# List of slots in two halves, the first gathers issued beside the later searches, TensorE given work ahead of their end, the last expert's rows signalled by halves

## The reference, cut to what matters

```python
cap = int(CAP_FACTOR * T / E)                          # 140
topp, topi = jax.lax.top_k(probs, TOPK)
score = jnp.where(routed, probs, -jnp.inf)
idx = jnp.argsort(-score, axis=0)[:cap].T              # 32 lists of 140 token numbers
xe = xf[idx]                                           # gather
up = jnp.einsum('eci,eji->ecj', xe, w_up)
gate, upv = jnp.split(up, 2, axis=-1)
ye = jnp.einsum('ecj,eoj->eco', silu(gate) * upv, w_down)
out = jnp.zeros((T, C)).at[idx.reshape(-1)].add((w[..., None] * ye).reshape(-1, C))
```

## Time and profile before

| what | us |
|---|---|
| median of three timed runs | 810.26 |
| profiled execution, its time | 806.49 |
| its span | 804.7 |
| the searches (L669) | 21.9 |
| last search to the turn of expert 0's rows | 7.35 |
| turn of expert 0's rows to turn of expert 1's | 8.87 |
| turn of expert 1's rows to that of expert 2's | 7.95 |
| end of the last matmul of the last expert to the last add issued | about 5 |

### The profile page before, as it was taken

How to read it: one execution, slowest core, us unless ns; L and a number is a source line. 1 busy time by engine, 2 the same in 40 slices (tenths; PEclk the granted TensorE clock), 3 DMA queues, 4 the chain that set the end, 5 groups by cost and what they waited for, 6 DMA issues and landing times.

```text
span 804.7 us, 17481 instructions
## 1 busy us (share of the span) xinstructions
PE 675.4 (84%) x5198; PEld 532.4 (66%) x5198; DVE 507.6 (63%) x1371; ACT 393.2 (49%) x1590; POOL 322.9 (40%) x339
## 2 busy tenths in 40 slices
PE   7899999999999999998866111079999999999993
PEld 4456666666666666665643100069999999999992
DVE  5665777867777786766578888925454545454541
ACT  1467686867768686777732563012222222222220
POOL 3343453534445353441101000035656565656542
PEclk8999999999999999999976555579999999999997
DMA  5600020202002020101014200018898988898931
GB/s 163 238 1 24 25 70 2 70 26 69 24 23 70 2 69 24 46 1 46 2 41 133 74 1 0 0 33 258 245 274 253 266 243 272 251 274 234 278 60 14
DMA packets 57422, 84.44 MB, mean 105 GB/s; under 512 B 11282, under 2 KB 28304, under 8 KB 57360
## 3 DMA queue, kind: packets, MB, share of 16 engines
q1 hardware_dynamic: 47168, 73.04, 27.7%
q0 software_dynamic: 9216, 9.76, 7.4%
q10 hardware_dynamic: 976, 0.96, 0.4%
HBM read 71.04 MB, written 12.69 MB: 104 GB/s over the span
## 4 chain that ended last, share of the span: by engine, by line
PE 60%; DVE 17%; ACT 14%; issue 4%; DMA 2%; SPq 1%; POOL 1%; ACTq 0%; DVEq 0%; POOLq 0%
PE pair L808 19%; PE bank L818 10%; ACT arena L1083 7%; PE pair L1385 6%; DVE arena L1254 5%; PE pair L1394 3%; PE bank L1413 3%; PE bank L1352 3%; PE pair L1380 3%; DVE arena L669 3%; PE bank L1340 2%; PE bank L1345 2%; PE bank L828 2%; ACT arena L489 2%; PE bank L1364 1%
## 5 line engine op out<-in xcount | busy, mean ns | idle before, releaser
L1083 ACT ACTIVATE arena<-pair,arena 112x112 f32<-112x112 f32 x512 | 175.5, 365 | 72.3 <-DVE arena L1254 68.5
L808 PE MATMUL pair<-arena,we 128*128 128x140 f32 x1024 | 139.9, 285 | 0.7 <-ACT arena L729 0.6
L772 DVE SCALAR_TENSOR_TENSOR arena<-arena,pair 128x140 f32<-128x140 f32 x160 | 47.7, 298 | 133.8 <-issue 73.6
L714 POOL DMA_INDIRECT rows_out<-arena,slot_row x64 | 94.4, 1475 | 92.7 <-DVE arena L761 75.0
L808 PEld LDWEIGHTS pair<-arena,we 128*128 128x128 f32 x1024 | 130.1, 192 | 1.8 <-issue 1.8
L737 ACT ACTIVATE arena<-pair 128x140 f32<-128x140 f32 x160 | 45.9, 287 | 149.0 <-PE pair L808 99.0
L705 POOL DMA_INDIRECT arena<-rows,slot_row x64 | 62.5, 977 | 120.8 <-issue 120.8
L1083 ACT ACTIVATION_READ_ACCUMULATOR arena<-pair,arena 112x1 f32 x512 | 110.0, 215 | 0.0
L818 PE MATMUL bank<-arena,we 128*128 128x140 f32 x512 | 83.3, 286 | 0.0
L1254 DVE TENSOR_REDUCE arena<-pair 112x8 f32<-112x896 f32 x64 | 69.4, 1085 | 19.8 <-PE pair L1385 19.0
L1394 PEld LDWEIGHTS pair<-tab,arena 112*112 112x112 f32 x512 | 52.0, 134 | 30.6 <-issue 28.7
(11 more groups left out here) (188 smaller groups left out, 1178.5 us busy)
## 6 DMA issues: line engine op xcount, KB each, us to landing
we<-w_experts_in SPq DMA_DIRECT2D x192, 256.0 KB
wa<-w_adapters_in SPq DMA_DIRECT2D x16, 384.0 KB
arena<-ctx_in SPq DMA_DIRECT2D x8, 448.0 KB, 4.4
arena<-x_in SPq DMA_DIRECT2D x8, 448.0 KB, 3.8
rows_out<-arena SPq DMA_DIRECT2D x8, 448.0 KB, 3.3
rows<-arena SPq DMA_DIRECT2D x8, 448.0 KB, 3.4
arena<-rows,slot_row POOLq DMA_INDIRECT x64
rows_out<-arena,slot_row POOLq DMA_INDIRECT x64
```

Source lines behind the costliest of these rows:

```text
L714: nc.gpsimd.indirect_dma_start(d["out"], bass.IndirectOffsetOnAxis(ap=slot_row[:, h, e:e + 1], axis=0), yr[e % 2][:, h, :], None, compute_ ...
L772: signal(dve, nc.vector.scalar_tensor_tensor(gs[m % 2], th[m % 2], 1.0, banks[m % 4][:, 0:CAP], ALU.add, ALU.mult), s_gs, n + 1)
L808: last = nc.tensor.matmul(banks[m % 4][:, part * CAP:(part + 1) * CAP], w[:, col0:col0 + 128], xet[j % 2][:, c, :], start=(c == 0), stop=( ...
L1083: last = nc.scalar.activation(pr[s % 2][:, j, :], banks[BS[s % 4]][0:T, j * T:(j + 1) * T], ACT.Exp, bias=nmx[s // 2 % 2][:, s % 2, j:j + ...
```

## The change

`HALF` is 72, nine of the 18 searches. After the ninth, VectorE turns the first 72 columns into token numbers and signals `s_found`; TensorE adds them up into bank 5; two searches later VectorE writes the first half of `slot_row` and signals `s_slot`. GpSimd then issues the gathers of the first halves of experts 0 to 3, and after the second signal the second halves of the same four. The second half of the list goes into bank 6 and takes the same steps after the last search. Each search now scans only up to its own numbers (`place[:, 0:end]`, 904 to 1040 columns). Three searches (`WAKE`) before the end VectorE signals `s_wake`, on which TensorE runs two of the large matmuls; behind the second half of the list it runs five (`WARM // 2 - 1`) where it ran three. In `add` the two waits change places, and for the last expert each half of the rows is signalled on its own.

```diff
-        pe.wait_ge(s_found, 1)
         for h in range(2):
-            last = nc.tensor.matmul(banks[5][0:HC, h * NE:(h + 1) * NE], row_id[:, h * HC:(h + 1) * HC],
-                                    tab[:, TAB["chunk"]][:, 0:NE], start=True, stop=True)
-        last.then_inc(s_placed, 1)
+            if h == 1:
+                pe.wait_ge(s_wake, 1)
+                keep_warm(2, ident[0:T, 0:T], tab[0:T, 0:NT])
+            pe.wait_ge(s_found, h + 1)
+            nc.tensor.matmul(banks[5 + h][0:HC, 0:NE], row_id[:, h * HC:(h + 1) * HC],
+                             tab[:, TAB["chunk"]][:, 0:NE], start=True, stop=True).then_inc(s_placed, 1)
...
+        def rows_at(h):
+
+            some = slice(h * HALF, (h + 1) * HALF)
+            link(nc.vector.scalar_tensor_tensor(row_id[:, some], at[:, some], tab[:, TAB["first"]], shift[:, some], ALU.add,
+                                                ALU.subtract))
+            link(nc.vector.scalar_tensor_tensor(row_id[:, some], at[:, some], float(CHB * T), row_id[:, some], ALU.is_lt,
+                                                ALU.mult))
+            dve.sem_inc(s_found, 1)
+
+        def slots(h):
+            dve.wait_ge(s_placed, h + 1)
+            nc.vector.tensor_scalar(slot_row[:, h, :], banks[5 + h][0:HC, 0:NE], tab[0:HC, TAB["spare"]][:, h:h + 1], None,
+                                    ALU.add).then_inc(s_slot, 1)
+
         for i in range(FINDS):
             some = slice(i * FIND, (i + 1) * FIND)
-            last = nc.vector.max_index(at[:, some], place[:, CHB * T + i * FIND:CHB * T + (i + 1) * FIND], place)
+            end = CHB * T + (i + 1) * FIND
+            last = nc.vector.max_index(at[:, some], place[:, end - FIND:end], place[:, 0:end])
+            if (i + 1) * FIND == HALF:
+                link(last)
+                rows_at(0)
+            elif (i + 1) * FIND == HALF + 2 * FIND:
+                slots(0)
+            elif i == FINDS - 1 - WAKE:
+                link(last)
+                dve.sem_inc(s_wake, 1)
         link(last)
...
+        rows_at(1)
+        slots(1)
...
-            pool.wait_ge(s_yr, e + 1)
-            plain(pool)
             wait(pool, s_added, 32 * e)
             plain(pool)
+            pool.wait_ge(s_yr, e + 1)
+            plain(pool)
             for h in range(2):
+                if e == NE - 1 and h == 1:
+                    pool.wait_ge(s_yr, NE + 1)
                 nc.gpsimd.indirect_dma_start(d["out"], bass.IndirectOffsetOnAxis(
...
-        for e in range(4):
-            fetch(e)
+        for h in range(2):
+            pool.wait_ge(s_slot, h + 1)
+            for e in range(4):
+                fetch(e, h)
...
-            last.then_inc(s_yr, 1)
+                if halves or h == 1:
+                    last.then_inc(s_yr, 1)
...
-        pe.wait_ge(s_slot, 1)
-        keep_warm(WARM // 4, ident[0:T, 0:T], tab[0:T, 0:NT])
+        pe.wait_ge(s_slot, 2)
+        keep_warm(WARM // 2 - 1, ident[0:T, 0:T], tab[0:T, 0:NT])
```

More of the change, by code:

```diff
@@ L33 @@
 PAD = FIND * FINDS
+HALF = PAD // 2
+WAKE = 3
+assert HALF % FIND == 0 and HC <= HALF
 NCH, CHB = 4, NB // 4
@@ L448, in program @@
     s_counted, s_base, s_placed, s_found = sem("chosen_counted"), sem("bases"), sem("row_ids"), sem("rows_found")
-    s_slot = sem("slot_rows")
+    s_slot, s_wake = sem("slot_rows"), sem("search_nearly_done")
     s_cand, s_sc = sem("bounds"), sem("scalar_candidates")
@@ L665, in routing_vector @@
         link(nc.vector.tensor_tensor(place[:, 0:CHB * T], pg, pe_, ALU.add))
+        def rows_at(h):
[9 more added lines that the diff above has]
+                                    ALU.add).then_inc(s_slot, 1)
         for i in range(FINDS):
             some = slice(i * FIND, (i + 1) * FIND)
-            last = nc.vector.max_index(at[:, some], place[:, CHB * T + i * FIND:CHB * T + (i + 1) * FIND], place)
-        link(last)
[L671 to L679, removed]
+            end = CHB * T + (i + 1) * FIND
[8 more added lines that the diff above has]
+                dve.sem_inc(s_wake, 1)
+        link(last)
+        rows_at(1)
+        slots(1)
     s_xet, s_xrt, s_up, s_th, s_hh, s_yt, s_yts, s_yw, s_yr = (sem(n) for n in (
@@ L700, in experts_pool, with fetch @@
         pool.wait_ge(s_fo, 16 * 2)
[L701 to L706, removed]
+        def fetch(e, h):
+            nc.gpsimd.indirect_dma_start(xr[e % 4][:, h, :], None, d["rows"], bass.IndirectOffsetOnAxis(
+                ap=slot_row[:, h, e:e + 1], axis=0)).then_inc(s_xr[e % 4], 16)
         def add(e):
+            wait(pool, s_added, 32 * e)
+            plain(pool)
             pool.wait_ge(s_yr, e + 1)
             plain(pool)
-            wait(pool, s_added, 32 * e)
-            plain(pool)
             for h in range(2):
+                if e == NE - 1 and h == 1:
+                    pool.wait_ge(s_yr, NE + 1)
                 nc.gpsimd.indirect_dma_start(d["out"], bass.IndirectOffsetOnAxis(
@@ L722, in experts_pool @@
             if e + 4 < NE:
-                fetch(e + 4)
+                fetch(e + 4, 0)
+                fetch(e + 4, 1)
         pool.wait_ge(s_added, 32 * NE)
@@ L755, in experts_vector, with turned @@
     def experts_vector(dve, link):
-        def turned(e, j):
+        def turned(e, j, halves=False):
             dve.wait_ge(s_yw, e + 1)
@@ L788, in experts_vector @@
                 expert(4 * i + j, j, False)
-        turned(NE - 1, 3)
+        turned(NE - 1, 3, True)
     def experts_tensor(pe):
```

## The result

The changed kernel took 807.31 us in the median of 8 runs (804.70 to 810.42), the kernel before 810.41 in the median of its own 8. The ratio is 0.9962 with a 95% interval from 0.9945 to 0.9978: 3.1 us less, between 1.8 and 4.5. 808.4 had been forecast.

The account below looks back on a forecast made before the run. Experts bound by TensorE, searches by VectorE; gains lie in searches, the way to first rows, the clock's second fall and tail. Against the median 810.26: 0.45 + 1.0 + 0.45 = 1.9, so 808.4 us; range 805.9 to 810.6.

Parts of the forecast that it names:

- The searches and the list: Shorter scans save 1.28 us, work between searches adds 1.1, the end saves 0.6: slots complete 0.75 us earlier.
- The gathers: Early gathers leave one behind the last signal: expert 0's rows land 2.2 us earlier, most of it hidden behind five matmuls.
- rival 3: Searches and gathers disturb each other: slots 3.8 us later, time about 811.9; chance 0.04.
- Rival 4: First half not early because of another GpSimd wait; expert 0's second gather comes fifth, about 811.5; chance 0.03.
- The turn of expert 0's rows: Before the first expert, TensorE's five large matmuls delay the turn: 531.3, 0.45 us earlier than before.
- u: Time from the start of the five large matmuls to the clock's rise: 3.35 to 3.9 us, allowed 2.5 to 6.
- The formula: End of the five large matmuls behind the list: 525.75 + 3.73 + u/2.
- rival 2: Five matmuls outlast the rows; with first up blocks still at half clock, +1.0 us, 811.2; chance 0.10.
- The fall of the clock: Between the large matmuls and the second expert the clock no longer falls: 1.6 us gained against the profiled execution.
- The discount to 1.0: The clock-fall gain counted as 1.0 us against the median, since not each run of before need have the fall.
- The tail: Behind the last expert, the first add waits only for the first half of rows: 0.45 us saved, bounds 0 and 0.5.
- Rival 1: Early matmuls raise the clock before the five run: 3.7 to 4.3 us less, time 806.2; chance 0.27.

Follow-up runs that it names:

- before_tail: The kernel before with only the edit of the last expert's rows and the swapped waits; single run, last-step-to-first-add 1.33 us instead of 1.82, no timed ratio.
- the paced matmuls: Changed kernel with one large matmul signalled by each of the 12th to 17th searches instead of two at once; 804.90 and 806.10 us, ratios 0.9937 and 0.9946 to before.

## Why the prediction was right, point by point

**The searches and the list.** 0.75 us had been worked out to the start of the large matmuls; it was 0.64 (24.00 -> 23.36 us after the first search). The scan's 1.28 came as 1.27, and what is added less what is saved as 0.63 instead of 0.5.

**The gathers.** They ran beside the searches, ended before the second half, and disturbed nothing: seven searches took 8.32 us with them and 8.32 without. So rival 3, a port conflict, falls (its price, 3.8 us on top of the forecast, would have been 812.2 and not 811.9); this agrees with the Trainium skill's exemption for VectorE instructions with one SBUF input ("SBUF — State Buffer", Who interferes with whom). The second halves' first gather started sooner than forecast, 0.30 us after the slots instead of 1.0. None of it reached the turn: the rows were there 3.9 us earlier, so the matmuls hid all of it, where the prediction had them hide most. Rival 4 falls too: the first early gather started 1.08 us after the first slots (517.89 -> 518.97).

**The turn of expert 0's rows: the mis-sized step.** I had u, the time from the start of the five to the rise, at 3.35 to 3.9 us and the turn 0.45 us earlier than before. In three profiles u was 5.8 to 6.5 and the turn 0.8 to 1.2 us later than before. The formula held: 525.75 + 3.73 + u/2 becomes 527.95 + 3.73 + 5.92 / 2 = 534.64, and the turn started at 534.72. The u I took from two rows were two draws of a wide spread, and both early: where the rise came during the large matmuls behind the list, u was 3.3 to 6.5 in eight profiles. 6.5 is even outside the 2.5 to 6 that I allowed. So this term had the wrong sign, and the half of rival 2 that concerns the turn came true.

**The fall of the clock.** 1.6 us forecast, 8.99 - 7.26 = 1.73 measured, in each of the changed kernel's profiles. The 1.9 that the prediction also names was too much: it scaled 0.95 us for 8 records to 2.86 for 24, and 24 at full clock take 3.10, so there it was 4.77 - 3.10 = 1.67. That it need not be in each run of before was right in kind: in the profile of `before_tail` there was no rise ahead of the turn at all and turn to turn took 8.95. The discount to 1.0 was too large if half level is as common in the first expert as that; two out of two profiles of a kernel with three matmuls and the old order of gathers had it, and they agree to the end: 302.2 us, and 302.1 with the 0.49 of the tail edit added back.

**The tail.** 0.45 forecast, 0.49 measured, alone and in the whole.

**The sum.** In the profiles: -0.9 (turn) + 1.73 + 0.49 = 1.3 us, and first search to end says the same (302.2 - 300.9). The timed runs say 3.1, 2.4 and 2.4 (ratios 0.38, 0.30 and 0.29% under one), with intervals that go down to 1.8, 0.9 and 0.3. So the forecast of 1.9 was nearer to the timed gain than a sum with the measured terms would have been, and that is luck: the turn went the other way, the fall gave more than the 1.0 counted, and 1 to 2 us of the timed gain have no source in the profiles. The 0.38% is also past the 0.3% for which I had given 0.37. This part stays open. Two repeats have 1.3 us inside their intervals, the first comparison hasn't; the five matmuls in the kernel before show the same gap (2.0 timed, 0.5 in the profile); and the profiles show too few executions to tell how often the clock rises earlier.

**Rival 1** (the early matmuls raise the clock before the five) wasn't seen, and their removal cost nothing measurable. What it promised, 3.7 to 4.3 us less, is what the paced matmuls reached and passed: 5.1 and 4.4 us. **Rival 2** happened in its first half in all three profiles: the five outlast the rows. It didn't turn the sign of the time because its second half, first up blocks at half clock, never came with it: the long matmuls end at full clock and the turn follows at once.

## What to carry to other kernels

Read the stretch in front of a TensorE-bound stage by the granted clock first: work that only wakes the engine should be paced so that the clock is up when the data arrives, and should run up to the first real matmul without a pause; together this gave 3.3 us at the turn. Behind wake-up work at half clock the earlier list and transfer moved the turn by 0.3 us at most, and the same transfer was worth 3.1 us once the clock was up; so test the two together, not one after the other. A bound on the moment of a clock's rise needs several executions, not two rows of one. And where the code ahead of a change varies by more than the change is worth, measure from a mark behind it: to the end the three profiles of the changed kernel agree within 0.4 us, their first searches start 3.9 us apart.

## What the runs showed of the hardware that was not expected

- 3.33 us of large matmuls at half clock, 1.9 us of pause and 5.92 us more of them: the clock rose only at the end of this. In the kernel before 3.35 us of the same work were enough. When the rise comes isn't fixed by the work alone.
- With a pause of 1.2 us in front of the turn, on top of the 0.6 us behind it, the clock that the paced matmuls had held for 10 us was lost (one profile); with the 0.6 us alone it stayed in both profiles of the paced kernel.
- A search costs 1.27 us / (18 x 68 columns) = 1.04 ns a column, about the same as an elementwise step (1.05).
- GpSimd started its gather 0.30 us after the slots when it had issued one 4 us before, and about 1.1 after 92 to 102 us of waiting.
- One stall of ScalarE of 3.54 us in one execution out of two of the same kernel.
